# Three steps of cross-attention's first sequence, issued at ticks 65 to 67 of self-attention's loop

## The reference

```
x = x + L0_attn(layernorm(x))                  # five state-space layers, then causal self-attention, 16 heads of 64
x = x + L0_xattn(layernorm(x), ctx, ctx)       # cross-attention, 16 heads of 16: the part the change is about
x = x + L0_ffn(layernorm(x))                   # top 2 of 8 experts
x = x + L1_attn(layernorm(x))
x = x + L1_xattn(layernorm(x), ctx, ctx)
x = x + L1_ffn(layernorm(x))
```

```
Q = query @ W_q.T + b_q ; K = key @ W_k.T + b_k ; V = value @ W_v.T + b_v
qk = einsum('bhqd,bhkd->bhqk', Q, K) * scale
attn = softmax(qk) ; out = einsum('bhqk,bhkd->bhqd', attn, V) @ W_o.T + b_o
```

## Time and profile before

| | |
|---|---|
| median of three runs | 1288.87 us |
| the profiled execution's own time | 1288.29 us |
| its span on the core | 1286.5 us |
| PE busy | 1139.6 us, 89% of the span |
| VectorE, ScalarE, GpSimd busy | 838.1, 646.4, 663.0 us |
| mean granted TensorE clock | 0.952 of full speed |
| self-attention's tail, ticks 64 to 72 | about 704 to 722 us after the start |
| cross-attention after that | 720.39 us (first scores) to 870 us |

### The profile page before, as it was taken

The page is one execution under the profiler, slowest core; times in us unless marked ns, Lnnn a source line. Parts: engine busy times, 40 slices in busy tenths (PEclk is TensorE's granted clock), DMA queues, the critical chain, the costliest instruction groups (busy, mean ns, idle before and its releaser), DMA issues. The chain is left out here.

```text
span 1286.5 us, 21156 instructions
## 1 busy us (share of the span) xinstructions
PE 1139.6 (89%) x6835; PEld 891.7 (69%) x6835; DVE 838.1 (65%) x1886; ACT 646.4 (50%) x1892; POOL 663.0 (52%) x705
## 2 busy tenths in 40 slices
PE   3999999999997999999988599975599999996984
PEld 3788888888875787787867477754366666655862
DVE  6888898888882666565677588864432343324795
ACT  2555555555542655555554488872122444224873
POOL 3275766757562224334253667751266655642664
PEclk9999999999997999999999899996699999997995
DMA  4002001010000000000010122404432222322001
GB/s 150 16 2 77 3 22 56 17 61 17 17 1 1 1 2 1 1 1 1 2 50 18 58 105 77 199 2 140 133 47 45 44 47 42 47 33 69 1 21 47
DMA packets 38077, 53.72 MB, mean 42 GB/s; under 512 B 8320, under 2 KB 32896, under 8 KB 36448
## 3 DMA queue, kind: packets, MB, share of 16 engines
q1 hardware_dynamic: 29248, 42.28, 9.6%
q0 software_dynamic: 8736, 10.25, 5.0%
HBM read 40.78 MB, written 11.74 MB: 41 GB/s over the span
## 5 line engine op out<-in xcount | busy, mean ns | idle before, releaser
L414 DVE SCALAR_TENSOR_TENSOR ssm_conv<-bank,conv_w,ssm_conv 128x508 f32<-128x508 f32 (+2 forms) x240 | 159.2, 728 | 10.0 <-ACT ssm_conv L350 10.0
L705 ACT ACTIVATE a_prob<-a_prob,a_neg_max 128x128 f32<-128x128 f32 x256 | 99.7, 391 | 129.8 <-DVE a_neg_max L751 129.8
L1468 PE MATMUL bank<-expert_raw,e_rows_t 128*128 x312 | 149.8, 604 | 1.2 <-ACT e_rows_t L1555 1.2
L303 PE MATMUL bank<-w_out,ssm_u 128*128 128x256 f32 x640 | 143.5, 383 | 0.0
L303 PEld LDWEIGHTS bank<-w_out,ssm_u 128*128 128x128 f32 x640 | 120.2, 190 | 17.6
L808 POOL TENSOR_TENSOR a_prob<-a_prob,a_inv 128x512 f32<-128x512 f32 x64 | 66.2, 1040 | 119.3 <-DVE a_inv L756 119.3
L1395 POOL DMA_INDIRECT x_rows<-e_y,e_index x39 | 62.8, 1611 | 76.9 <-ACT e_y L1583 73.2
L508 POOL TENSOR_TENSOR act_t_lo<-ssm_turned,act_t_hi 128x512 fp32r<-128x512 f32 x40 | 51.5, 1288 | 97.8 <-ACT ssm_turned L375 97.8
L1721 DVE COPY e_h_t<-bank 128x512 f32<-128x512 f32 x39 | 27.0, 692 | 105.3 <-PE bank L1477 105.3
L1098 ACT ACTIVATE x_prob<-bank,x_neg_max 128x128 f32<-128x128 f32 x256 | 89.6, 402 | 9.4 <-DVE x_neg_max L1075 9.4
L1468 PEld LDWEIGHTS bank<-expert_raw,e_rows_t 128*128 128x128 f32 x312 | 57.4, 194 | 43.1 <-issue 41.2
(11 more groups left out here) (327 smaller groups left out, 2996.2 us busy)
## 6 DMA issues: line engine op xcount, KB each, us to landing
expert_raw<-in_experts_laid SPq DMA_DIRECT2D x8, 1536.0 KB, 7.6
attn_raw<-in_attn_w_laid SPq DMA_DIRECT2D x4, 1024.0 KB, 7.4
w_in_raw<-in_L_attn_in_proj_w SPq DMA_DIRECT2D x5, 640.0 KB, 8.3
w_out<-in_L_attn_out_proj_w SPq DMA_DIRECT2D x5, 512.0 KB, 3.8
x_res<-in_x SPq DMA_DIRECT2D x4, 512.0 KB, 5.6
x_context<-in_ctx_t_laid SPq DMA_DIRECT2D x8, 256.0 KB, 3.4
z_rows<-cv SPq DMA_DIRECT2D x4, 512.0 KB, 2.9
x_rows<-x_res SPq DMA_DIRECT2D x4, 512.0 KB, 4.6
```

What stands on the lines that cost most here:

```text
L303: mm = pe.matmul(UWY[h][:, s * D:(s + 1) * D], u[:, g % 2, c, t:t + P], w_out[:, c, :], start=(c == 0), stop=(c == KI - 1))
L414: op = dve.scalar_tensor_tensor(out=acc, in0=xs, scalar=conv_w[:, c, TAPS - 1 - back:TAPS - back], in1=acc, op0=ALU.mult, op1=ALU.add)
L705: e = act.activation(prob[:, m % 4, i, :], prob[:, m % 4, i, :], ACT.Exp, bias=neg_max[:, m % 4, i:i + 1], accum_out=total[:, m % 4, i:i + 1])
L1468: mm = pe.matmul(bank[:, :], rows_t[:, t % 2, k, :], W[:, bass.ds(at + (column + k * FFN), FFN)], start=(k == 0), stop=(k == KD - 1))
```

## The change

A second table names ticks for the first sequence's scores (65), maxima (66) and exponentials (67). `early_turns` issues them there, all four groups each, and `turns` leaves that sequence out of these three phases. All other steps of the first sequence, `invert_sums` and `share_out` among them, keep their places after tick 72.

```diff
 LEAD = {72: 0}
+LED_TICKS = {"scores": (65,), "maxima": (66,), "exps": (67,)}
 
 def early_turns(m, phases):
-    return [(phase, n, 0) for phase in EARLY_TICKS if phase in phases for n in range(EARLY) if EARLY_TICKS[phase][n] == m]
+    pairs = [(phase, n, 0) for phase in EARLY_TICKS if phase in phases for n in range(EARLY) if EARLY_TICKS[phase][n] == m]
+    return pairs + [(phase, n, r) for phase in LED_TICKS if phase in phases for n, tick in enumerate(LED_TICKS[phase]) if tick == m
+                    for r in range(len(BY_SEQ[phase]))]
 
 def turns(phases, first, last):
...
         if phase in BY_SEQ:
-            places += [(at + BEAT * b, b, r, phase) for r, at in enumerate(BY_SEQ[phase]) for b in range(SEQS)]
+            led = len(LED_TICKS[phase]) if phase in LED_TICKS else 0
+            places += [(at + BEAT * b, b, r, phase) for r, at in enumerate(BY_SEQ[phase]) for b in range(led, SEQS)]
```

## The result

The changed kernel takes 1292.84 us, median of 12 runs (1290.70 to 1295.34), against 1288.88 us for the kernel before (12 runs, 1285.90 to 1291.59). The ratio is 1.0032, with the interval 1.0019 to 1.0044. That is +4.0 us. Predicted were +3.5 us and 1292.4 us, as a loss too small to count as slower. The profiled execution, the fastest of the twelve, took 1290.7 us for a span of 1288.9, with a mean granted clock of 0.949.

What follows compares the result with a forecast made beforehand. The path into the cross stage, ending in GpSimd's finishes and share_out, was taken as binding: 0.75 + 2.40 + 0.35 - 0 = +3.5 us, so 1292.4 us. Forecast range 1291.2 to 1293.9, over all cases 1288.6 to 1296.5.

Steps and rivals of the forecast that it cites:

- The path named: Into the cross stage: low splits, projections and residuals of U30 and U31, power, two finishes, share_out, transpositions.
- Scores, 0.75: PE, tick 65: scores delay self-attention's last transpositions and U29's residual by 0.75 us, bounds 0.22 to 1.07.
- Maxima, 2.40: VectorE, tick 66: four reductions in front of U30's low split delay it by 2.40 us, bounds 1.87 to 2.49.
- The clock, taken as 0: PE's low-clock stretch around U31's projection and the first cross work expected again: 0 us, bounds -2.57 to +0.60.
- Exponentials, 0.35: ScalarE, tick 67: sixteen exponentials hold up U31's high split, adding 0.35 us, bounds 0 to 1.2.
- The sign named for this step: In the profile after, exponentials on ScalarE from 714.8 to 720.2 us, U31's high split at once behind, without idle time.
- Removed work, 0: Scores, maxima and exponentials leaving the hole before the cross stage gain 0 us, bounds 0 to 0.18.
- A: Rival: idle time in the tail absorbs the moved work, at most the scores' 0.75 left, 1288.9 to 1289.6 us; 7 in 100.
- B: Rival: PE's clock stays up; 1286.1 us, 4 in 100 for not slower; head alone 1289.8 us, 7 in 100.
- C: Rival: clock stays low past 733 us, up to 6.4 us more per sequence; one gives 1298.8 us; 6 in 100.

Runs made afterwards that it cites:

- the second comparison: The changed kernel timed once more, no edit, against the kernel before: ratio 1.0047 (1.0030 to 1.0063).
- PE filled: Changed kernel plus unread transpositions of a constant in PE's idle time at ticks 68, 70 and 72; ratio to the kernel before 1.0042.
- the maxima alone: Kernel before plus four extra VectorE reductions at tick 66, result overwritten; scores, maxima and exponentials of the first sequence not moved; ratio 1.0038.
- the kernel without the exponentials: Changed kernel with exponentials back behind tick 72, scores still at 65 and maxima at 66; ratio to the kernel before 1.0040.
- the kernel with all steps at 69, 69 and 70: Changed kernel with scores and maxima moved to tick 69 and exponentials to tick 70; ratio to the kernel before 1.0008.

## Why the prediction was right, and where a step was not

The forecast held: +3.5 us, measured +4.0 (the interval is +2.4 to +5.7) and in the second comparison +6.1 (+3.9 to +8.1), whose middle lies above the forecast's own range of +2.3 to +5.0. The path named was the one that decided. That the sum came so near is in part luck: two of its terms were wrong with opposite signs, the clock by +1.02 and the exponentials by -0.35. Its steps, in the first profile of the changed kernel against the first of the kernel before:

- **Scores, 0.75.** U29's residual came 5.43 us after x_q_t's copy started, and 4.58 before: +0.85. PE waited 0.62 us for the copy and the scores held it for 1.08; the prediction's handover was 0.05 and the real one 0.14. Against the second profile of the kernel before, where this distance was 3.93, it is +1.50. In that one the copy came 1.25 us later (708.45 for 707.20), and GpSimd's probabilities, for which PE waited 0.85 us in the first, were there already. So the scores cost 0.85 us without the dip of the clock ahead of the copy, and 1.5 with it: PE, which there went straight on to the transpositions before, now waited 0.62 us for the copy as well. From U28's to U29's residual the change adds 0.86 us where both executions are without the dip (7.17 with PE filled, 6.31 in the first profile of before) and 1.51 where both have it (8.84 in the second profile of the changed kernel, 7.33 in the second of before).
- **Maxima, 2.40.** 3.92 us from U29's residual to U30's low split, and 1.53 before: +2.39, and 2.39 to 2.40 in every profile with the maxima there. The place in the list was the cause, as the kernel with the maxima alone and the one with maxima at tick 65 show.
- **The clock, taken as 0.** This step was mis-sized, and the +1.02 measured lies outside the bounds given for it (-2.57 to +0.60). The maxima delay the low split, and PE's idle time in front of U30's projection grew to 3.17 us. That was foreseen (0.78 + 2.40), but the low level was looked for in U31's projection and behind. It held through the whole of U30's projection: 3.76 us from low split to residual against 2.53, +1.23. U31's was then 2.92 against 3.13, -0.21. The sentence on the Trainium skill's page "TensorE: Matmul & The Clock Gate", Part 1, pointed the right way: longer idle time brought the low level earlier. The +1.2 for U30's projection stood in all four profiles with the maxima at tick 66 and no filling. What the clock cost in all did not: U31's projection took 3.76, 2.99, 2.92 and 2.64 us in these four, and 3.13 and 3.77 in the two of the kernel before. For the whole change the net is thus 0.1 to 1.0 us, by which pair of profiles is taken, and up to 1.9 for the maxima alone.
- **Exponentials, 0.35.** Their part was 0 in both profiles of the changed kernel, since the low clock made PE as late as ScalarE. The sign named for this step, a high split without idle time, was there and could not tell: engine and PE came free together. The kernel without the exponentials could. At full clock they do bind (+0.47 with PE filled). The two are not a sum: the later of two arrivals counts. The forecast counted the one that didn't bind and left out the one that did.
- **Removed work, 0.** Right. U31's residual to share_out is 6.55 us before and after, and the kernel with all steps at 69, 69 and 70 empties the hole for no gain that shows.

The sum by these rows: 0.85 + 2.39 + 1.23 - 0.21 + 0 = 4.26 us from x_q_t's copy to share_out, which is 24.11 - 19.85. In front of it the copy itself was 0.45 later by its own execution's clock, which makes 4.71 at share_out and 4.72 at the barrier. In this pair of profiles the whole delay passed through the cross stage, as the chain of waits and the full stretch had suggested. Against the second profile of the kernel before only 2.78 of 4.28 us are left at the barrier: from share_out to the barrier that one took 149.01 us, where the first took 147.50, with the same lists. So a single pair shows the passing only to about 1.5 us.

Of the rivals, A is refuted for this place and right for others: the tail absorbs the maxima at 65 and at 69, not at 66. B, that the clock helps, is refuted: it hurt. C did not come: the stretch from 737.30 on was granted 0.99.

"In front of the barrier goes into the total one for one" holds only on average. C differs by up to 4.2 us between executions, 409.41 to 413.62, and by 2.5 and 3.9 us between the two executions of the kernel before and of the changed one.

The rule of the Trainium skill's page "Perfetto Trace Analysis", Optimization Strategy, that interleaving regimes may help, was weighed as rival A or B. The runs say where it is true here: it cost 0.3 to 0.5% in front of the low split, nothing in idle places, and it paid (0.9977) only once the engine that set the start of the next stage, GpSimd, was reordered too.

## What to carry to other kernels

Ask what an inserted instruction stands in front of, not how idle its engine is: idle time behind it in an in-order list pays for it only up to the next instruction that was late already. Where two delays meet, take the later one and not their sum. And to shorten the gap between two stages, reorder the list of the engine that ends it (here GpSimd's finishes and share_out); feeding the others earlier gives nothing until that is done.

## What the hardware showed that was not expected

A delay on VectorE came back larger through TensorE's clock: 2.4 us of reductions, PE idle for 3.17 us, and the next twelve matmuls at 0.21 us spacing instead of 0.12, in all four profiles with this delay and no filling. Shorter idle time gave no fixed answer: after 2.39 to 2.40 us in front of U31's projection its matmuls began at the low level in two profiles of eight and at 2.4 GHz in the other six, some of them falling within it.

The stretch C falls into three groups: 409.4 to 409.9 us (five profiles), 411.2 to 412.2 (six) and 413.5 to 413.6 (two), whatever the kernel. The granted clock 40 to 60 us after the barrier goes with it in all 13: 0.83 to 0.85 in the first group, 0.77 to 0.81 in the second, 0.73 and 0.74 in the third. The 31 runs of the kernel before in one comparison lie at 1285.8 to 1288.9 (22) and 1291.0 to 1291.9 (9), with none between. Their mean granted clocks differ too: 0.952 to 0.954 in the lower group but for one run (0.949), 0.948 to 0.949 in the upper. Stretch C by itself is not that difference. The two profiled executions of the kernel before, with C at 411.95 and 409.41, took nearly the same time, 1288.29 and 1288.49 us, as the one with the short C had come to the barrier 2.7 us later. An estimate from their rows: an execution with both the late barrier and the long C would take 877.29 + 411.95 + 1.8 = 1291.0 us, and one with neither 874.55 + 409.41 + 1.8 = 1285.8 (1.8 is what an execution's time exceeds its span by). These are the values at which the two groups begin. That this is how they come about is not shown, as only one execution of a comparison has a trace.
